# First layer's maximum pass of a two-layer attention kernel: one maximum over two banks in place of two over one

## The chip, the cores and the metric

One core of a Trainium2 chip runs the whole program. The time is device microseconds (us) of one execution. The figures of the kernel before are three plain runs and one profiled execution; its trace has 75059 instructions.

## What is computed

Eight images of 64 x 64 positions with 64 channels go through two attention layers. For each image, with n = 4096 positions:

```
xf = x.reshape(b, n, c)
f = xf @ wf + bf;  g = xf @ wg + bg;  hh = xf @ wh + bh      # layer 0, f and g have 8 channels
s = einsum('bnk,bmk->bnm', g, f)
x = gamma * softmax(s) @ hh + x
q, k, v = projections of x with 64 channels each             # layer 1
x = gamma1 * softmax(q @ k^T) @ v + x
```

The softmax of layer 0 needs the maximum of each row of s before its exponentials. This kernel finds it in a pass of its own, the maximum pass, with a cheaper product (72 contraction rows instead of 75), and that pass is what the change is about.

## The kernel before, in words

PSUM is held as two tensors of four banks, each 128 partitions by 512 f32: score_banks and sum_banks. The work of layer 0 on one image is cut into NCH = 4 chunks (q = 0 to 3) of 1024 query positions. chunk0 on PE (L435), ACT (L591) and DVE (L734) walks a chunk in T = 32 steps (i = 0 to 31), each over 128 key positions. The order of every engine's instructions is written out by hand, and semaphores couple the engines.

One step on PE is, in order:

- scores0 (L380): two matmuls of 512 columns (L383) into two banks of score_banks. ACT then takes the exponential of the 1024 columns in one instruction (L600) into one of eight slots of e_whole.
- max_pass_tiles (L361): two matmuls of 512 columns (L366), each into its own bank of sum_banks (banks 2 and 3), for a chunk that comes later. DVE takes the maximum of each bank with block_max (L724, instruction at L727).
- values0 (L394): f32 matmuls (L401, recorded as four per step) that add the weighted values of step i - 5 (LAG0 = 5) into bank 0. In one step of four the row sums of that slot go to PE too (sum_of, L414, matmuls at L417, into bank 1); in the other three POOL adds the slot to a running sum (L289, L292).

The maximum pass has 8 tiles of 512 keys per block of 128 queries (ATN = 8), 64 per chunk; a step of the loop does tiles 2(i mod 4) and 2(i mod 4) + 1 of one block. A tile's matmul waits on the semaphore a_used, which DVE raises by one per maximum; GpSimd gives FREE_A = 4 credits at the start. In the loop only banks 2 and 3 are used (banks=2), in the pass ahead of the first image (L506 to L508 on PE, L809 to L813 on DVE, 80 tiles) all four banks (banks=4). DVE waits on a_ready, one per matmul.

Some steps are different:

- q = 0, i = 0 to 4: no values0, since the lag of 5 isn't filled. These steps are scores and maximum tiles alone. The first values0 is in step i = 5.
- q > 0: steps 0 to 4 carry the last five values of the chunk before. Step 5 has no values0. Step 6 has turn0 (L421): PE transposes the sums that ACT (v_sb, L589) and DVE (d_sb, L732) have copied, and DVE turns them into the attention output with attention0 (L761: L767, L768, L769) once it has done the maxima of step 6. Steps 7 and 8 have two values0 each, and the first waits for L769 since it writes bank 0 again.
- i = 23: DVE writes the row maxima of the next chunk with split_max (L749, five small instructions), after its maxima.
- i = 26 (MROW_AT): after values0, max_rows (L369) waits for every maximum issued so far and for split_max, and writes banks 2 and 3 with eight small matmuls (L376); ACT copies them out (L584).
- i = 27: the maximum tiles come last in the step, behind values0 and a wait for that copy (L459 to L461), so that the tiles of step 27 and of step 28 have only the two score matmuls of step 28 between them.

Layer 1 (scores1 L463, values1 L473, steps1 L546/L654/L875) has a maximum of 1024 columns over two banks per step already, in one DVE instruction (L880). It isn't touched.

Of the kernel before, what the change touches and what calls it, by code (L numbers as in the profile page):

```python
# [21 lines left out]
AX_X = mybir.AxisListType.X  # L22
ds = bass.ds

P = 128
BANK = 512
# [4 lines left out]
def attention_pair_kernel(nc, x, wf, bf, wg, bg, wh, bh, gamma0, wq, bq, wk, bk, wv, bv, gamma1, out):  # L31
    B, H, W, C = x.shape
    N = H * W
# [4 lines left out]
    CH = 2 * BANK  # L38
# [9 lines left out]
    RT = T // BPC  # L48
    ATN = N // BANK
    ATS = T * ATN  # L50
    U0 = 8
# [4 lines left out]

    FREE_ST, FREE_A, FREE_E0, FREE_S1, FREE_E1 = 2, 4, U0, 2, U1
    FREE = 1
# [16 lines left out]
    with ExitStack() as ctx:  # L75
# [239 lines left out]
        def _(pe):  # L315
# [44 lines left out]

            def max_pass_tiles(ahead, blk, js, banks=2):  # L361

                image, par, q = ahead
                for j in js:
                    pe.wait_ge(a_used, image * ATS + q * TILES + blk * ATN + j + 1 + FREE_A - banks)
                    nc.tensor.matmul(sum_banks[:, (2 + j % banks) % 4, :], g_tr[0:KS, par, ds(q * CH + blk * P, P)],  # L366
                                     f_tr[0:KS, par, j * BANK:(j + 1) * BANK], start=True, stop=True).then_inc(a_ready, 1)

# [62 lines left out]
            def after(image, par, q):  # L431

                return (image, par, q) if q < NCH else (image + 1, 1 - par, q - NCH)

            def chunk0(image, par, q):  # L435
# [3 lines left out]
                for i in range(T):  # L439
                    scores0(image, par, q, i)  # L440
                    if q == 0 and i == 0:
                        pe.wait_ge(y_ready, image * NCH + FREE)
                    tiles = range(2 * (i % 4), 2 * (i % 4) + 2)
                    if i < LAST:
# [12 lines left out]
                    if i == MROW_AT:  # L457
                        max_rows(after(image, par, q + 1), 2 * (MROW_AT - LAST + 1))
                    elif i == MROW_AT + 1:  # L459
                        pe.wait_ge(mrow_sb, image * NCH + q + 2)  # L460
                        max_pass_tiles(after(image, par, q + 2), (i - LAST) // 4, tiles)  # L461
# [44 lines left out]
            for chunk, blocks in ((0, BPC), (1, EARLY)):  # L506
                with pe.Fori(0, blocks) as blk:
                    max_pass_tiles((0, 0, chunk), blk, range(ATN), 4)  # L508
            max_rows((0, 0, 0), EARLY * ATN)
# [174 lines left out]
        def _(dve):  # L684
# [38 lines left out]

            def block_max(chunk, blk, js, banks=2):  # L724
                for j in js:
                    dve.wait_ge(a_ready, chunk * TILES + blk * ATN + j + 1)
                    nc.vector.reduce_max(tile_max[:, blk, j:j + 1], sum_banks[:, (2 + j % banks) % 4, :], AX_X  # L727
                                         ).then_inc(a_used, 1)

# [4 lines left out]
            def chunk0(image, par, q):  # L734
                ahead = image * NCH + q + 1
                for i in range(T):
                    tiles = range(2 * (i % 4), 2 * (i % 4) + 2)
                    if i < LAST:
                        block_max(ahead, EARLY + i // 4, tiles)
                    else:  # L740
                        block_max(ahead + 1, (i - LAST) // 4, tiles)
                    if q > 0 and i == LAG0:
                        copy_sums0(image, q - 1)
                    if q > 0 and i == TURN_AT:
                        attention0(image, q - 1)
                    if i == LAST - 1:
                        split_max(ahead, (par * NCH + q + 1) % (2 * NCH))
# [61 lines left out]
            with dve.Fori(0, BPC) as blk:  # L809
                block_max(0, blk, range(ATN), 4)  # L810
            split_max(0, 0)
            with dve.Fori(0, EARLY) as blk:
                block_max(1, blk, range(ATN), 4)  # L813
            START += 2 * LINK_PIECES + LINK_MAX
# [134 lines left out]
```

## Time and profile before

| | us |
|---|---|
| plain runs, median of 3 | 5068.23 |
| plain runs, lowest and highest | 5059.25, 5069.01 |
| profiled execution, its own time | 5049.6 |
| its span, first to last instruction | 5047.8 |
| mean granted TensorE clock in it | 0.943 of full speed |

The page's first part gives the busy time of each engine and its share of the span. PE is the tensor engine's matmuls, PEld its weight loads, which run beside matmuls. A line of the costliest groups reads: source line, engine, operation, output<-input, shapes, count, then busy us and mean ns of one, then the idle time in front of them and who ended it. A line of the timeline reads: start us, length us, engine, source line, operation, tiles, count of merged instructions, and in brackets the idle time before it and what released it. Matmul ends are modelled, so the start of the next one tells more than the length of one. A line of the windows reads: stretch, its length, busy us (and count) of PE, PEld, DVE, ACT and POOL, then PEclk, the granted TensorE clock as a share of full speed (full speed is 2.4 GHz, 0.5 is 1.2 GHz), the DMA share and GB/s.

### The profile page before, as it was taken

Reading aid. Unit: us, or ns where it says so; the run is one execution under the profiler, and the core shown is the slowest. Engines: PE = TensorE matmul, PEld = TensorE weight load, DVE = VectorE, ACT = ScalarE, POOL = GpSimd, SP = SyncE. Lnnn points to the kernel's source line nnn. Section 1 sums busy time; section 2 is a strip of 40 time slices with the busy share of each in tenths; the row PEclk is TensorE's granted clock in tenths of the full one; section 3 lists DMA queues with packets and bytes.
Section 4 is the critical chain, followed back from the end, with each engine's and each line's share of the span. In section 5 each row is a group of like instructions: output and inputs, shape, how many; then the busy total and the mean of one; then the engine's idle time right before and its main releaser. Section 6 shows DMA issues by size and latency. Waiting matters only on the chain.

```text
span 5047.8 us, 75059 instructions
## 1 busy us (share of the span) xinstructions
PE 4836.0 (96%) x21608; PEld 1511.7 (30%) x21608; DVE 3533.9 (70%) x6722; ACT 2755.7 (55%) x3752; POOL 1831.4 (36%) x821
## 2 busy tenths in 40 slices
PE   7999999999999999999999999999999999999999
PEld 3224222242222422233222422224222242222422
DVE  6566876678765787558866588665885568866687
ACT  2555655556555565546655466554664546655465
POOL 2772017710177003760037600475005740067300
PEclk6998999989999899998989989998998989999899
DMA  0000000000000000000000000000000000000000
GB/s 26 1 9 17 0 8 1 9 17 0 9 1 9 17 0 9 1 9 17 0 10 1 18 9 0 9 1 24 2 0 10 1 26 0 0 9 3 24 0 8
DMA packets 13506, 40.03 MB, mean 8 GB/s; under 512 B 2620, under 2 KB 2620, under 8 KB 10812
## 3 DMA queue, kind: packets, MB, share of 16 engines
q1 hardware_dynamic: 13244, 36.78, 2.4%
q8 instruction: 135, 2.21, 0.2%
q14 instruction: 127, 1.04, 0.1%
HBM read 19.99 MB, written 8.39 MB: 6 GB/s over the span
## 4 chain that ended last, share of the span: by engine, by line
PE 61%; DVE 24%; issue 11%; ACT 2%; DVEq 1%; SPq 0%; ACTq 0%; DMA 0%
PE sum_banks L401 20%; DVE chunk_max L880 15%; PE score_banks L383 10%; PE sum_banks L366 9%; PE score_banks L468 5%; PE score_banks L469 4%; PE sum_banks L480 3%; PE sum_banks L417 3%; PE score_banks L541 2%; PE score_banks L340 2%; DVE tile_max L727 2%; DVE exp_bias L883 2%; ACT e_whole L659 1%; DVE inv_sum L862 1%; PE score_banks L325 1%
## 5 line engine op out<-in xcount | busy, mean ns | idle before, releaser
L727 DVE TENSOR_REDUCE tile_max<-sum_banks 128x1 f32<-128x512 f32 (+1 forms) x2128 | 1363.4, 686 | 914.3 <-PE sum_banks L366 914.1
L292 POOL TENSOR_TENSOR e_sum<-e_sum,e_whole 128x1024 f32<-128x1024 f32 x704 | 1655.4, 2351 | 429.7 <-ACT e_whole L600 409.2
L600 ACT ACTIVATE e_whole<-score_banks,no_bias 128x1024 f32<-128x1024 f32 x1024 | 1141.4, 1115 | 1105.2 <-PE score_banks L383 1103.1
L659 ACT ACTIVATE e_whole<-score_banks,exp_bias,down 128x1024 f32<-128x1024 f32 x1024 | 1233.3, 1204 | 764.7 <-DVE exp_bias L883 764.7
L880 DVE TENSOR_REDUCE chunk_max<-score_banks 128x1 f32<-128x1024 f32 x1024 | 1251.2, 1222 | 227.1 <-PE score_banks L469 212.9
L401 PE MATMUL sum_banks<-e_whole,proj 128*64 128x512 f32 x4096 | 1109.2, 627 | 27.0 <-DVE att L769 27.0
L480 PE MATMUL sum_banks<-e_whole,v_scaled 128*64 128x512 f32 x4096 | 1095.2, 617 | 6.6 <-DVE v_scaled L870 6.6
L289 POOL TENSOR_TENSOR e_sum<-e_whole 128x1024 f32<-128x1024 f32 x32 | 75.2, 2349 | 2231.3 <-ACT e_whole L600 2231.3
L468 PE MATMUL score_banks<-k_high,q_split 128*128 128x512 f16 x2048 | 800.4, 391 | 70.7 <-ACT e_whole L659 38.8
L469 PE MATMUL score_banks<-k_low,q_split 128*128 128x512 f16 x2048 | 790.3, 386 | 0.0
L366 PE MATMUL sum_banks<-f_tr,g_tr 72*128 72x512 bf16 x2128 | 693.2, 400 | 30.6 <-DVE tile_max L727 15.8
L383 PE MATMUL score_banks<-g_tr,f_tr 75*128 75x512 bf16 x2048 | 642.0, 396 | 12.1 <-issue 11.0
L468 PEld LDWEIGHTS score_banks<-k_high,q_split 128*128 (+1 forms) x2048 | 200.0, 98 | 1025.7 <-ACT e_whole L659 674.4
L401 PEld LDWEIGHTS sum_banks<-e_whole,proj 128*64 128x64 f32 x4096 | 214.3, 136 | 470.8 <-issue 437.3
L480 PEld LDWEIGHTS sum_banks<-e_whole,v_scaled 128*64 128x64 f32 x4096 | 207.5, 135 | 453.8 <-issue 453.8
L383 PEld LDWEIGHTS score_banks<-g_tr,f_tr 75*128 75x128 bf16 x2048 | 130.8, 99 | 659.0 <-ACT e_whole L600 464.9
L366 PEld LDWEIGHTS sum_banks<-f_tr,g_tr 72*128 72x128 bf16 (+1 forms) x2128 | 209.5, 100 | 396.1 <-DVE tile_max L727 140.8
L883 DVE TENSOR_SCALAR exp_bias<-chunk_max,neg_down 128x1 f32<-128x1 f32 x1024 | 219.2, 214 | 36.1
L469 PEld LDWEIGHTS score_banks<-k_low,q_split 128*128 (+1 forms) x2048 | 203.6, 99 | 126.9 <-issue 9.5
L659 ACT ACTIVATION_READ_ACCUMULATOR e_whole<-score_banks,exp_bias,down 128x1 f32 x1024 | 196.2, 192 | 0.0
L417 PE MATMUL sum_banks<-e_whole,ones_w 128*32 128x256 f32 x2048 | 164.6, 393 | 0.0
L541 PE MATMUL score_banks<-x_tr,w1s 65*128 65x512 f32 x128 | 111.9, 1069 | 12.3 <-DVE w1s L843 12.3
(100 smaller groups left out, 2074.3 us busy)
## 6 DMA issues: line engine op xcount, KB each, us to landing
x_in<-in_x_dram SPq DMA_DIRECT2D x19, 1024.0 KB, 4.9
out_dram<-x_mid SPq DMA_DIRECT2D x32, 256.0 KB, 2.2
k_high<-k_high SPq DMA_DIRECT2D x32, 128.0 KB, 2.2
k_low<-k_low SPq DMA_DIRECT2D x32, 128.0 KB, 2.2
gammas<-in_L_conv_gamma_dram SPq DMA_DIRECT2D x2, 0.5 KB
w<-in_L_conv_wg_dram SPq DMA_DIRECT2D x1, 2.0 KB
w<-in_L_conv_bg_dram SPq DMA_DIRECT2D x1, 0.0 KB
w<-in_L_conv_wf_dram SPq DMA_DIRECT2D x1, 2.0 KB
```

The costliest lines, as they stand in the source:

```text
L292: nc.gpsimd.tensor_tensor(acc, acc, e_whole[:, i % U0, :], ALU.add).then_inc(e_added, 1)
L366: nc.tensor.matmul(sum_banks[:, (2 + j % banks) % 4, :], g_tr[0:KS, par, ds(q * CH + blk * P, P)], f_tr[0:KS, par, j * BANK:(j + 1) * BANK ...
L383: mm = nc.tensor.matmul(score_banks[:, 2 * (i % 2) + h, :], f_tr[0:KM, par, i * P:(i + 1) * P], g_tr[0:KM, par, q * CH + h * BANK:q * CH + ...
L401: mm = nc.tensor.matmul(sum_banks[half * C:(half + 1) * C, 0, :], proj[:, par, i, GFW:PW], e_whole[:, i % U0, half * BANK:(half + 1) * BAN ...
L468: nc.tensor.matmul(bank, q_split[:, ds(i * P, P)], k_high[:, col:col + BANK], start=True, stop=False)
L469: mm = nc.tensor.matmul(bank, q_split[:, ds(i * P, P)], k_low[:, col:col + BANK], start=False, stop=True)
L480: mm = nc.tensor.matmul(sum_banks[half * C:(half + 1) * C, j, :].rearrange("c (k n) -> c k n", n=P), v_scaled[:, u // NCH, j, :], half_of_ ...
L600: nc.scalar.activation(e_whole[:, i % U0, :].rearrange("p (a n) -> p a n", a=2), score_banks[:, 2 * (i % 2):2 * (i % 2) + 2, :], ACT.Exp, ...
L659: nc.scalar.activation(e_whole[:, u, :].rearrange("p (a n) -> p a n", a=2), score_banks[:, 2 * (u % 2):2 * (u % 2) + 2, :], ACT.Exp, bias= ...
L727: nc.vector.reduce_max(tile_max[:, blk, j:j + 1], sum_banks[:, (2 + j % banks) % 4, :], AX_X).then_inc(a_used, 1)
L880: chain.link(nc.vector.reduce_max(chunk_max[:, odd, j:j + 1], score_banks[:, 2 * (u % 2):2 * (u % 2) + 2, :] .rearrange("p a n -> p (a n)" ...
L883: nc.vector.tensor_scalar(exp_bias[:, u:u + 1], chunk_max[:, odd, j:j + 1], neg_down[:, 0:1], None, ALU.mult).then_inc(bias_ready, 1)
```

## The change

The unit of the maximum pass becomes a pair of banks. PE writes two matmuls into a pair and raises a_ready once, after the second; both stand behind one wait on a_used. DVE takes one maximum over the 1024 columns of the pair and raises a_used once. ATN falls from 8 to 4 and FREE_A from 4 to 2. In the loop there is one pair (pairs=1, banks 2 and 3), so each pair of matmuls waits for the maximum of the step before; in the pass ahead of the first image there are two pairs (pairs=2, all four banks).

```diff
@@ -46,7 +46,7 @@
     TR = BANK // P
     RND = T // TR
     RT = T // BPC
-    ATN = N // BANK
+    ATN = N // CH
     ATS = T * ATN
     U0 = 8
     U1 = 2 * NCH
@@ -54,7 +54,7 @@
     LAG1 = 7
     STEPS0, STEPS1 = NCH * T, T * NCH
 
-    FREE_ST, FREE_A, FREE_E0, FREE_S1, FREE_E1 = 2, 4, U0, 2, U1
+    FREE_ST, FREE_A, FREE_E0, FREE_S1, FREE_E1 = 2, 2, U0, 2, U1
     FREE = 1
 
     EARLY = U0 // 4
@@ -358,13 +358,17 @@
                         mm.then_inc(ready, 1)
 
 
-            def max_pass_tiles(ahead, blk, js, banks=2):
+            def max_pass_tiles(ahead, blk, js, pairs=1):
 
                 image, par, q = ahead
                 for j in js:
-                    pe.wait_ge(a_used, image * ATS + q * TILES + blk * ATN + j + 1 + FREE_A - banks)
-                    nc.tensor.matmul(sum_banks[:, (2 + j % banks) % 4, :], g_tr[0:KS, par, ds(q * CH + blk * P, P)],
-                                     f_tr[0:KS, par, j * BANK:(j + 1) * BANK], start=True, stop=True).then_inc(a_ready, 1)
+                    pe.wait_ge(a_used, image * ATS + q * TILES + blk * ATN + j + 1 + FREE_A - pairs)
+                    pair = 1 - j % pairs
+                    for h in range(2):
+                        mm = nc.tensor.matmul(sum_banks[:, 2 * pair + h, :], g_tr[0:KS, par, ds(q * CH + blk * P, P)],
+                                              f_tr[0:KS, par, (2 * j + h) * BANK:(2 * j + h + 1) * BANK],
+                                              start=True, stop=True)
+                    mm.then_inc(a_ready, 1)
 
             def max_rows(ahead, tiles_ahead):
 
@@ -440,7 +444,7 @@
                     scores0(image, par, q, i)
                     if q == 0 and i == 0:
                         pe.wait_ge(y_ready, image * NCH + FREE)
-                    tiles = range(2 * (i % 4), 2 * (i % 4) + 2)
+                    tiles = [i % 4]
                     if i < LAST:
                         max_pass_tiles(after(image, par, q + 1), EARLY + i // 4, tiles)
                     elif i != MROW_AT + 1:
@@ -455,7 +459,7 @@
                     elif i >= LAG0 and (q == 0 or i > TURN_AT):
                         values0(image, par, q, i - LAG0)
                     if i == MROW_AT:
-                        max_rows(after(image, par, q + 1), 2 * (MROW_AT - LAST + 1))
+                        max_rows(after(image, par, q + 1), MROW_AT - LAST + 1)
                     elif i == MROW_AT + 1:
                         pe.wait_ge(mrow_sb, image * NCH + q + 2)
                         max_pass_tiles(after(image, par, q + 2), (i - LAST) // 4, tiles)
@@ -505,7 +509,7 @@
                 pe.wait_ge(gt_sb, (image + 1) * NCH)
             for chunk, blocks in ((0, BPC), (1, EARLY)):
                 with pe.Fori(0, blocks) as blk:
-                    max_pass_tiles((0, 0, chunk), blk, range(ATN), 4)
+                    max_pass_tiles((0, 0, chunk), blk, range(ATN), 2)
             max_rows((0, 0, 0), EARLY * ATN)
             def image_steps(image, par):
                 for q in range(NCH):
@@ -721,11 +725,12 @@
                     nc.vector.tensor_copy(half_of_blocks(r, 1), score_banks[C:P, r, :]
                                           .rearrange("c (k n) -> c k n", n=P)).then_inc(xt_dve[layer], 1)
 
-            def block_max(chunk, blk, js, banks=2):
+            def block_max(chunk, blk, js, pairs=1):
                 for j in js:
+                    pair = 1 - j % pairs
                     dve.wait_ge(a_ready, chunk * TILES + blk * ATN + j + 1)
-                    nc.vector.reduce_max(tile_max[:, blk, j:j + 1], sum_banks[:, (2 + j % banks) % 4, :], AX_X
-                                         ).then_inc(a_used, 1)
+                    nc.vector.reduce_max(tile_max[:, blk, j:j + 1], sum_banks[:, 2 * pair:2 * pair + 2, :]
+                                         .rearrange("p a n -> p (a n)"), AX_X).then_inc(a_used, 1)
 
             def copy_sums0(image, q):
                 dve.wait_ge(pv0_done, (image * NCH + q + 1) * T + FREE_E0)
@@ -734,7 +739,7 @@
             def chunk0(image, par, q):
                 ahead = image * NCH + q + 1
                 for i in range(T):
-                    tiles = range(2 * (i % 4), 2 * (i % 4) + 2)
+                    tiles = [i % 4]
                     if i < LAST:
                         block_max(ahead, EARLY + i // 4, tiles)
                     else:
@@ -807,10 +812,10 @@
                 assert chain.n == LINK_PIECES
             rebase(START + 2 * LINK_PIECES)
             with dve.Fori(0, BPC) as blk:
-                block_max(0, blk, range(ATN), 4)
+                block_max(0, blk, range(ATN), 2)
             split_max(0, 0)
             with dve.Fori(0, EARLY) as blk:
-                block_max(1, blk, range(ATN), 4)
+                block_max(1, blk, range(ATN), 2)
             START += 2 * LINK_PIECES + LINK_MAX
 
             def image_steps(image, par):
```

## Rows read from the trace of the kernel before

**Rows 1.** page, busy time of each engine

```profile
PE 4836.0 (96%) x21608; PEld 1511.7 (30%) x21608; DVE 3533.9 (70%) x6722; ACT 2755.7 (55%) x3752; POOL 1831.4 (36%) x821
```

**Rows 2.** page, costliest groups: the one-bank maximum and layer 1's two-bank maximum

```profile
L727 DVE TENSOR_REDUCE tile_max<-sum_banks 128x1 f32<-128x512 f32 (+1 forms) x2128 | 1363.4, 686 | 914.3 <-PE sum_banks L366 914.1
...
L880 DVE TENSOR_REDUCE chunk_max<-score_banks 128x1 f32<-128x1024 f32 x1024 | 1251.2, 1222 | 227.1 <-PE score_banks L469 212.9
```

**Rows 3.** timeline, an ordinary step of a chunk at full clock

```profile
755.74 0.60 PE L366 MATMUL sum_banks<-f_tr,g_tr 72*128 72x512 bf16 x2
...
756.16 1.29 DVE L727 TENSOR_REDUCE tile_max<-sum_banks 128x1 f32<-128x512 f32 x2 [0.69 <-PE sum_banks L366]
...
756.27 1.08 PE L401 MATMUL sum_banks<-e_whole,proj 128*64 128x512 f32 x4
...
757.51 0.32 PEld L366 LDWEIGHTS sum_banks<-f_tr,g_tr 72*128 72x128 bf16 x2
757.72 0.60 PE L366 MATMUL sum_banks<-f_tr,g_tr 72*128 72x512 bf16 x2
```

**Rows 4.** timeline, the pass ahead of the first image

```profile
62.00 4.28 DVE L727 TENSOR_REDUCE tile_max<-sum_banks 128x512 f32 x7 [1.00 <-PE sum_banks L366]
62.74 0.10 PEld L366 LDWEIGHTS sum_banks<-f_tr,g_tr 72*128 x1 [0.73 <-DVE tile_max L727]
62.75 0.39 PE L366 MATMUL sum_banks<-f_tr,g_tr 72*128 72x512 bf16 x1 [0.24 <-DVE tile_max L727]
```

**Rows 5.** timeline, steps without values, first image, low clock

```profile
114.36 1.06 PE L366 MATMUL sum_banks<-f_tr,g_tr 72*128 72x512 bf16 x2
...
115.03 1.29 DVE L727 TENSOR_REDUCE tile_max<-sum_banks 128x1 f32<-128x512 f32 x2 [3.79 <-PE sum_banks L366]
...
116.07 1.06 PE L366 MATMUL sum_banks<-f_tr,g_tr 72*128 72x512 bf16 x2
...
123.88 1.98 PE L401 MATMUL sum_banks<-e_whole,proj 128*64 128x512 f32 x4
```

**Rows 6.** timeline of PE, the same steps of the last image, full clock

```profile
4434.62 0.60 PE L366 MATMUL sum_banks<-f_tr,g_tr 72*128 72x512 bf16 x2 [1.15 <-DVE x_mid L917]
...
4441.56 0.65 PE L401 MATMUL sum_banks<-e_whole,proj 128*64 128x512 f32 x2
```

**Rows 7.** timeline, steps 5 to 7 of a chunk with q > 0

```profile
815.08 0.60 PE L366 MATMUL sum_banks<-f_tr,g_tr 72*128 72x512 bf16 x2
...
815.49 1.29 DVE L727 TENSOR_REDUCE tile_max<-sum_banks 128x1 f32<-128x512 f32 x2 [1.69 <-PE sum_banks L366]
...
816.70 0.41 DVE L732 COPY d_sb<-sum_banks 128x256 f32<-128x256 f32 x1
...
817.03 1.28 DVE L727 TENSOR_REDUCE tile_max<-sum_banks 128x1 f32<-128x512 f32 x2
```

**Rows 8.** timeline, the same place further on

```profile
819.88 3.62 PE L401 MATMUL sum_banks<-e_whole,proj 128*64 128x512 f32 x8 [1.12 <-DVE att L769]
...
824.40 1.94 PE L401 MATMUL sum_banks<-e_whole,proj 128*64 128x512 f32 x8
```

**Rows 9.** timeline, steps 26 to 28 of a chunk

```profile
790.12 1.29 DVE L727 TENSOR_REDUCE tile_max<-sum_banks 128x1 f32<-128x512 f32 x2 [0.69 <-PE sum_banks L366]
...
791.54 0.63 PE L376 MATMUL sum_banks<-ident_b,g_stack 128*75 128x128 bf16 x8 [0.23 <-DVE tile_max L727]
...
793.98 2.48 DVE L727 TENSOR_REDUCE tile_max<-sum_banks 128x1 f32<-128x512 f32 x4 [2.57 <-PE sum_banks L366]
...
795.64 1.08 PE L401 MATMUL sum_banks<-e_whole,proj 128*64 128x512 f32 x4
```

**Rows 10.** windows of 20 us from an image's first value matmul (images 0, 6, 7)

```profile
123.88:143.88 20.00, 20.00 (x63) 4.39 (x63) 8.71 (x14) 7.06 (x7) 12.45 (x6) 0.67 0.00 0
...
3824.67:3844.67 20.00, 20.00 (x51) 4.05 (x52) 6.79 (x12) 5.85 (x6) 10.54 (x5) 0.51 0.00 0
4441.56:4461.56 20.00, 20.00 (x94) 5.12 (x94) 12.28 (x20) 10.46 (x10) 18.37 (x9) 1.00 0.00 1
```

## The prediction

> **What bounds the kernel now.** I read the page's busy times first: PE is busy 96% of the span and DVE 70% [rows 1]. So the change, which takes work off DVE and none off PE, has nothing to win where PE never waits. The costliest groups give the two prices of a maximum: 686 ns for 512 columns, and in layer 1, which has the new shape already, 1222 ns for 1024 [rows 2]. The timeline of an ordinary step shows what matters most. PE starts the two tile matmuls at 755.74 and again at 757.72, a step of 1.98 us with PE issuing all the way, and DVE starts the first maximum 0.42 us after the first matmul, ends the pair 1.29 us later and then sits idle 0.69 us for PE [rows 3]. In layer 0 PE sets the time and DVE follows. A lighter DVE is worth nothing there; a PE made to wait costs all of the wait.
>
> **What the change does to the coupling.** Two things. The maximum starts after the second matmul, one issue spacing later (0.22 us at full clock, 0.43 us at half). And the loop keeps one pair of banks, so both matmuls of a step wait for the whole maximum of the step before, where the first one waited only for the first half. Pair against pair, start to end, DVE goes from 1.29 to 1.22 us, and since it starts 0.22 us later its pair ends 0.15 us later than now.
>
> The way round is then: first matmul, 0.22 to the second, 0.42 to the start of the maximum, 1.22 for it, then the release. In the pass ahead of the first image a maximum begins at 62.00 and lasts 0.68 us, and the weight load that waited for it starts at 62.74, its matmul at 62.75 [rows 4]: 0.06 for the release, 0.01 to the matmul. Sum 1.93 us at full clock. At half clock the first matmul of a pair to the first maximum is 0.67 us [rows 5], so the way round is 0.43 + 0.67 + 1.22 + 0.07 = 2.39 us. Wherever two tile pairs follow each other on PE in less than that, PE now stands still for the difference.
>
> **Ordinary steps: nothing, by 0.05 us.** They are 1.98 us apart, the way round is 1.93. The cover is the value matmuls between (1.0 us). Steps with row sums, and all steps with values at half clock, are longer still. Some 18 of 32 steps in each of the 32 chunks stand on this margin, nearly 600; if the way round were 0.05 us over the step, it would cost 30 us. I take nothing and keep 30 for the range. At i = 23 DVE's five small instructions follow the maximum; step 24 carries row sums, which cover them.
>
> **Steps 0 to 5 of q = 0 (eight times).** No values lie between the pairs of steps 0 to 5, five gaps. At half clock the pairs start 1.71 us apart, and 9.52 us pass from the first pair to the first value matmul [rows 5]. Now each gap is 2.39: 5 x 0.68 = +3.4 us. Seven of the eight images fall to half clock in or before these steps; I price them all so: 23.8 us. The last image stayed at full clock and took 6.94 us [rows 6]. With pairs 1.93 us apart PE would stand still for more than half of each gap, where it now stands still for a third of 1.2 us, and I expect the clock to fall as in the others: two gaps at 1.93, three at 2.39, 1.0 to the values, about 12.0 in all, +5.0 us. Below: if the clock held, 5 x (1.93 - 1.2) = +3.6.
>
> What follows in that image goes slow too. In the 20 us behind the first value matmul the clock averages 0.67 in the first image, 0.51 in the seventh and 1.00 in the last [rows 10]; the mean of all eight such windows is 0.80, so they hold 82 us at half clock, 11.7 for each of the seven that fell. Eight value matmuls take 3.62 us slow and 1.94 fast [rows 8], so a slow us wastes 0.46: +5.4 us for the last image. For the others no net change, though each image draws its length anew (2 to 20 us).
>
> **Steps 5 to 7 of q > 0 (24 times).** Step 5 has no values. The second maximum of step 5 ends at 816.78, DVE's copy of the sums and the two maxima of step 6 follow, the latter from 817.03 to 818.31 [rows 7], then L767 to L769, and the value matmuls at 819.88, after 1.12 us of idle PE that L769 ends [rows 8]. Now: the maximum of step 5 from 815.49 + 0.22 = 815.71 to 816.93; tiles of step 6 at 817.00 and 817.22; maximum 817.64 to 818.86. That is 0.55 us later on the chain that PE already waits for: 24 x 0.55 = +13.2 us. Queued behind the waiting tiles are the turn's transposes, whose inputs are ready by then, and the scores of step 7; ACT has room.
>
> **Step 26 (32 times).** max_rows waits for all maxima: they end at 791.41, L376 starts at 791.54 [rows 9]. All maxima now end 0.15 later: +4.8 us. **Steps 27 and 28 (32 times).** Only two score matmuls lie between their tiles. Already now both tiles of step 28 wait, and the value matmuls start at 795.64. Now: maximum from 793.98 + 0.22 = 794.20 to 795.42, tiles 795.49 and 795.71, and the values 0.31 later, as in an ordinary step [rows 3], at 796.02 against 795.64 [rows 9]: 32 x 0.38 = +12.2 us.
>
> **Pass ahead of the first image.** DVE is the bound: seven maxima take 4.28 us, a spacing of 0.60 [rows 4]. Two pairs of banks remain, so work overlaps. A 1024 maximum would be spaced by 1.22 less the overlap of 0.08, 1.14; by the way round at half clock, a pair for each of two, 2.39 / 2 = 1.19. Against 1.20 to 1.21: between -2.5 and 0 for 40 pairs. I take -1.0, since most of the stretch is at half clock. The Trainium skill, Perfetto Trace Analysis, section Optimizing Scalar/DVE Operations, gives about 125 ns of DVE time per PSUM instruction; by it 40 fewer instructions would give 5 us and the sum would be 4 lower. The rows say 0.06 us, since two maxima overlap by more than that.
>
> **Clock falls inside chunks.** At one of the 24 places above (the one of rows 8) the clock was at half for the first eight value matmuls, 1.68 us lost. PE now waits longer there; from one in 24 I go to three, +3.4, and hold 0 and 24 x 1.68 = 40 as the ends.
>
> **Sum.** 23.8 + 5.0 + 5.4 + 13.2 + 4.8 + 12.2 - 1.0 + 3.4 = +66.8 us, against the profiled execution's own 5049.6: 5116.4. The median of plain runs is 18.6 above that execution. I read part of that as the last image's luck, so the 5.4 and the 1.6 by which it costs more than the others don't come on top of the median: 5068.2 + 59.8 = **5128.0 us**, 1.2% slower.
>
> **Rivals.**
>
> 1. *The margin in ordinary steps is not there* (a longer maximum in layer 0, a later release). For: 0.05 us is two or three digits of the trace's last place, and 600 steps hang on it. Against: layer 1's duration has little spread and the restart of a waiting matmul costs 0.01. Price 30 us: 5158. In the same direction speaks the Trainium skill, Perfetto Trace Analysis, section Matmuls: independent groups should rotate through banks so that the evacuation overlaps the next matmuls, which the loop no longer does. Chance 0.14.
>
> 2. *The clock falls at most places with q > 0.* Price 40 - 3.4: 5165. For: one fell already. Against: 23 didn't, with 1.12 us of idle each. Chance 0.08.
>
> 3. *Stalls within slow stretches are half paid for*: the clock comes back at its own time whatever PE has done, so the 3.4 us per image replace slow work. Price: 27 x 0.46 = 12 less, 5116. Chance 0.15.
>
> 4. *Not slower.* One mechanism: slow clock. The profiled run averages 0.943, about 575 us at half clock. PE's longer waits shift when it rises; the gain is 0.46 us for each slow us saved, so from 130 us saved on it cancels the 60: 5068 or less. The stretches behind the images' starts hold only 82 us, worth 38, so these alone don't reach it; it would need the stretches between the layers too. Chance 0.05.
>
> That the code would not do what it says I exclude: with pairs=1 the pair is always banks 2 and 3, and the credits (2, and one pair held back) admit one maximum at a time.
>
> **How the numbers follow.** The forecast has 0.58, rival 3 0.15, rivals 1 and 2 0.22 together, rival 4 0.05. The range from 5096 (rival 3, no clock falls, luck of 15 us with the lengths) to 5165 (rival 1 or 2 alone) leaves out rival 4 and the sum of 1 and 2. A measurement of this kernel tells about 0.2%, 10 us, from no change. Rival 4 splits into faster by more, 0.03, and within, 0.02, to which the low tail of the forecast adds 0.01; slower by more has the rest, 0.94.
>
> **What would show it.** One L727 per step of about 1.22 us, 1064 in all. In ordinary steps L366 still 1.98 apart, with the weight load starting 0.05 or less ahead of its matmul instead of 0.21. Gaps of 2.4 us between pairs at the start of every image, the last too. From the tiles of step 5 to the first values of step 7, 5.35 us for 4.80 [rows 7, 8]. From the start of the first maximum of step 27 to the values of step 28, 1.82 us for 1.66, and 0.15 more ahead of L376. Wrong if steps of 2.0 us and more appear (rival 1), or if the mean clock rises.

## The result and the profile after

The changed kernel takes **5183.56 us** (median of 4 runs, 5159.24 to 5195.01) where the kernel before took 5063.74 in the same session: a ratio of **1.0235**, 95% interval 1.0207 to 1.0263. The forecast was 5128.0 in a range of 5096 to 5165. The sign was right; the loss is twice the forecast's (119.8 us for 59.8), and the time lies outside the range.

The profiled execution of the changed kernel took 5174.86 us, its span is 5172.9 (5047.8 before) and the mean granted clock 0.932 (0.943). Its page, busy time of each engine and three of the costliest groups (columns: busy us, mean ns of one, idle before them and what ended it):

```profile
PE 4888.8 (95%) x21608; PEld 1508.9 (29%) x21608; DVE 3488.7 (67%) x5658; ACT 2753.4 (53%) x3752; POOL 1830.4 (35%) x821
...
L732 DVE TENSOR_REDUCE tile_max<-sum_banks 128x1 f32<-128x1024 f32 (+1 forms) x1064 | 1300.8, 1224 | 1078.9 <-PE sum_banks L368 1078.0
...
L405 PE MATMUL sum_banks<-e_whole,proj 128*64 128x512 f32 x4096 | 1137.5, 642 | 42.5 <-DVE att L774 42.5
...
L368 PE MATMUL sum_banks<-f_tr,g_tr 72*128 72x512 bf16 x2128 | 683.3, 404 | 94.5 <-DVE tile_max L732 87.7
```

DVE has 1064 maxima of 1.22 us in place of 2128 [rows 1, 2], as forecast. They are busy 63 us less (1300.8 for 1363.4), but DVE as a whole only 45 us less: some of the saving went into another instruction, shown below. PE's waits went up. Its busy time went up by 53 us with the same 21608 matmuls, which is slow clock (700 us of the span at half clock instead of 579, by the clock records).

**An ordinary step** (timeline, after; start, us, engine, line). It answers to [rows 3].

```profile
775.62 0.60 PE L368 MATMUL sum_banks<-f_tr,g_tr 72*128 72x512 bf16 x2
776.26 1.23 DVE L732 TENSOR_REDUCE tile_max<-sum_banks 128x1 f32<-128x1024 f32 x1 [0.76 <-PE sum_banks L368]
...
777.54 0.17 PEld L368 LDWEIGHTS sum_banks<-f_tr,g_tr 72*128 72x128 bf16 x2 [0.27 <-DVE tile_max L732]
777.61 0.60 PE L368 MATMUL sum_banks<-f_tr,g_tr 72*128 72x512 bf16 x2
```

The tiles are 1.99 and 1.98 us apart as before, and the weight load now starts 0.07 ahead of its matmul instead of 0.21 (0.05 or less was forecast). The margin held.

**The start of an image** (timeline of PE, after, second image). It answers to [rows 5, 6].

```profile
746.77 0.60 PE L368 MATMUL sum_banks<-f_tr,g_tr 72*128 72x512 bf16 x2 [1.15 <-DVE x_mid L922]
...
748.69 0.61 PE L368 MATMUL sum_banks<-f_tr,g_tr 72*128 72x512 bf16 x2 [0.89 <-DVE tile_max L732]
...
750.62 1.04 PE L368 MATMUL sum_banks<-f_tr,g_tr 72*128 72x512 bf16 x2 [0.89 <-DVE tile_max L732]
...
752.97 1.03 PE L368 MATMUL sum_banks<-f_tr,g_tr 72*128 72x512 bf16 x2 [0.47 <-DVE tile_max L732]
755.33 1.03 PE L368 MATMUL sum_banks<-f_tr,g_tr 72*128 72x512 bf16 x2 [0.47 <-DVE tile_max L732]
757.68 1.03 PE L368 MATMUL sum_banks<-f_tr,g_tr 72*128 72x512 bf16 x2 [0.47 <-DVE tile_max L732]
```

The gaps are 1.92 and 1.93 at full clock and 2.35 at half, as worked out (1.93 and 2.39).

**Where the 125.1 us of span went.** I took the length of every one of the 1024 steps in both traces (from a step's scores to the next step's) and subtracted.

| place | forecast | measured |
|---|---|---|
| ordinary steps | 0 | 0.0 |
| the five gaps at the start of q = 0 (steps 1 to 5 by this count) | 28.8 | 28.5 |
| step 0 (-2.0) and steps 6 to 12 (+15.3) of q = 0, more half clock | 5.4 | 13.4 |
| steps 5 to 8 of q > 0, clock falls included | 16.6 | **60.5** |
| step 26 | 4.8 | 4.9 |
| steps 27 and 28 | 12.2 | 11.8 |
| pass ahead of the first image | -1.0 | +1.9 |
| start of the kernel up to that pass | 0 | +5.6 |
| everything else | 0 | -1.5 |
| sum | 66.8 | 125.1 |

One row is far off: steps 5 to 8 of q > 0, where the values wait for a chain of small instructions on DVE (the reciprocal L772, the multiply L773 and the attention output L774). The 24 places are of two kinds. Timeline of the changed kernel, first a chunk of the bad kind (POOL's two additions are rows of POOL's own timeline):

```profile
837.03 2.35 POOL L292 TENSOR_TENSOR e_sum<-e_sum,e_whole 128x1024 f32<-128x1024 f32 x1 [0.62 <-ACT e_whole L604]
...
839.18 0.20 DVE L772 RECIPROCAL inv_sum<-sum_banks 128x8 f32<-128x8 f32 x1
839.42 2.41 DVE L773 TENSOR_SCALAR inv_gam<-inv_sum,gammas 128x8 f32<-128x8 f32 x1
839.46 2.34 POOL L292 TENSOR_TENSOR e_sum<-e_sum,e_whole 128x1024 f32<-128x1024 f32 x1
841.86 0.69 DVE L774 TENSOR_TENSOR att<-sum_banks,inv_gam 128x512 f32<-128x512 f32 x1
...
842.70 3.25 PE L405 MATMUL sum_banks<-e_whole,proj 128*64 128x512 f32 x8 [2.77 <-DVE att L774]
```

and the next chunk, of the good kind:

```profile
913.12 2.35 POOL L292 TENSOR_TENSOR e_sum<-e_sum,e_whole 128x1024 f32<-128x1024 f32 x1 [0.62 <-ACT e_whole L604]
...
915.27 0.20 DVE L772 RECIPROCAL inv_sum<-sum_banks 128x8 f32<-128x8 f32 x1
915.51 0.23 DVE L773 TENSOR_SCALAR inv_gam<-inv_sum,gammas 128x8 f32<-128x8 f32 x1
915.56 2.39 POOL L292 TENSOR_TENSOR e_sum<-e_sum,e_whole 128x1024 f32<-128x1024 f32 x1
915.77 0.69 DVE L774 TENSOR_TENSOR att<-sum_banks,inv_gam 128x512 f32<-128x512 f32 x1
...
916.61 1.94 PE L405 MATMUL sum_banks<-e_whole,proj 128*64 128x512 f32 x8 [0.59 <-DVE att L774]
```

The same instruction, a multiply of 8 values in each of 128 partitions by a scale, takes 0.23 us or 2.41. When it takes 2.41 it ends 0.03 after the end of POOL's addition, which started 0.04 behind it. PE waits 2.77 us instead of 0.59 for the values, and the values then run slow (3.25 for 1.94). The windows of 8 us around the two places (PE, PEld, DVE, ACT, POOL busy with counts, then the granted clock):

```profile
837.00:845.00 8.00, 4.60 (x18) 1.96 (x20) 6.25 (x7) 2.48 (x3) 4.69 (x2) 0.81 0.00 1
911.00:919.00 8.00, 6.29 (x33) 2.48 (x30) 4.95 (x7) 3.72 (x4) 6.25 (x3) 1.00 0.01 2
```

The clock is at full (2.4 GHz) throughout the good one and at half (1.2) in part of the bad one. Over the chunks with q > 0, half clock rose from 3.4 us to 68.3, and all of it lies behind 12 of the 13 long multiplies. At the 13th the multiply takes 2.41 us and PE waits 2.77 as well, and the clock stays at full (two lines of the timeline, then the window of 8 us around them):

```profile
4147.93 2.41 DVE L773 TENSOR_SCALAR inv_gam<-inv_sum,gammas 128x8 f32<-128x8 f32 x1
...
4151.22 1.51 PE L405 MATMUL sum_banks<-e_whole,proj 128*64 128x512 f32 x6 [2.77 <-DVE att L774]
```

```profile
4145.50:4153.50 8.00, 4.59 (x22) 1.90 (x23) 6.26 (x7) 2.50 (x3) 4.68 (x2) 1.00 0.01 2
```

At the other 12 the clock falls 1.7 to 3.8 us after the multiply has begun, never before it.

The multiply was too long in the kernel before, too. Kernel before, the same chain as timeline (it lies between [rows 7] and [rows 8]), and then the row of the multiply's line over the whole run (ns, min/median/max):

```profile
816.63 2.35 POOL L292 TENSOR_TENSOR e_sum<-e_sum,e_whole 128x1024 f32<-128x1024 f32 x1 [0.62 <-ACT e_whole L600]
818.23 0.20 DVE L767 RECIPROCAL inv_sum<-sum_banks 128x8 f32<-128x8 f32 x1
818.46 0.55 DVE L768 TENSOR_SCALAR inv_gam<-inv_sum,gammas 128x8 f32<-128x8 f32 x1
...
819.04 0.69 DVE L769 TENSOR_TENSOR att<-sum_banks,inv_gam 128x512 f32<-128x512 f32 x1
819.06 2.35 POOL L292 TENSOR_TENSOR e_sum<-e_sum,e_whole 128x1024 f32<-128x1024 f32 x1
```

```profile
L768 DVE TENSOR_SCALAR inv_gam<-inv_sum,gammas x32: 230/549/554, 202.8 to 4722.3; 128x8 f32<-128x8 f32 x32
```

It starts 1.83 us into POOL's addition and ends 0.03 behind it (816.63 + 2.35 = 818.98, 818.46 + 0.55 = 819.01). The next addition starts 0.60 after the multiply did, so there was a hole of 0.05 us (819.01 to 819.06) that it always went through. It took 0.55 at all 24 places with q > 0 and 0.23 at the 8 places behind an image's last chunk, where POOL adds nothing (its last addition had ended 7 us earlier). In the changed kernel it arrives 0.03 behind the end of one addition and 0.05 ahead of the next, and it was held at 13 of the 24 places.

### The profile page after: what moved, and what is told of

The parts are those of the page before. It is cut to its first block, busy times and chain, and to the rows that moved or that the text cites. A ratio compares the mean times of both kernels' runs of the same rounds, so it can differ in the third digit from the quotient of the medians.

```text
span 5172.9 us, 71767 instructions
## 1 busy us (share of the span) xinstructions
PE 4888.8 (95%) x21608; PEld 1508.9 (29%) x21608; DVE 3488.7 (67%) x5658; ACT 2753.4 (53%) x3752; POOL 1830.4 (35%) x821
## 4 chain that ended last, share of the span: by engine, by line
PE 61%; DVE 25%; issue 10%; ACT 2%; DVEq 1%; SPq 0%; ACTq 0%; DMA 0%
PE sum_banks L405 20%; DVE chunk_max L885 15%; PE sum_banks L368 10%; PE score_banks L387 10%; PE score_banks L472 5%; DVE tile_max L732 4%; PE score_banks L473 3%; PE sum_banks L421 3%; PE sum_banks L484 3%; PE score_banks L545 2%; PE score_banks L340 2%; DVE exp_bias L888 2%; PE score_banks L528 1%; ACT e_whole L663 1%; DVE inv_sum L867 1%
## 5 line engine op out<-in xcount | busy, mean ns | idle before, releaser
L732 DVE TENSOR_REDUCE tile_max<-sum_banks 128x1 f32<-128x1024 f32 (+1 forms) x1064 | 1300.8, 1224 | 1078.9 <-PE sum_banks L368 1078.0
L405 PE MATMUL sum_banks<-e_whole,proj 128*64 128x512 f32 x4096 | 1137.5, 642 | 42.5 <-DVE att L774 42.5
L368 PEld LDWEIGHTS sum_banks<-f_tr,g_tr 72*128 72x128 bf16 (+1 forms) x2128 | 181.9, 100 | 461.3 <-DVE tile_max L732 334.5
L279 POOL TENSOR_TENSOR g_stack<-piece,ones_b 128x768 bf16<-128x768 bf16 x30 | 54.0, 1800 | 200.4 <-DVE piece L795 200.4
```

The source lines that it names most:

```text
L368: mm = nc.tensor.matmul(sum_banks[:, 2 * pair + h, :], g_tr[0:KS, par, ds(q * CH + blk * P, P)], f_tr[0:KS, par, (2 * j + h) * BANK:(2 * j ...
L405: mm = nc.tensor.matmul(sum_banks[half * C:(half + 1) * C, 0, :], proj[:, par, i, GFW:PW], e_whole[:, i % U0, half * BANK:(half + 1) * BAN ...
```

## The experiments

The theory to be tested is that this hold makes the excess. Its rivals: the chain is simply later and every 0.1 us of it is paid; or the slow clock comes first and the long steps from it.

**First group: take the multiply out of either kernel, and delay it in the kernel before.** `pair_fused` is the changed kernel with gamma folded into the ones that PE multiplies for the row sums (so gamma must not be 0), `single_fused` the same edit on the kernel before:

```diff
+            chain.link(nc.vector.reciprocal(inv_gamma0[:, :], gammas[:, 0:1]))
+            nc.vector.tensor_scalar(ones_w[:, :], ones_w[:, :], inv_gamma0[:, 0:1], None, ALU.mult).then_inc(w_ready, 1)
...
-                chain.link(nc.vector.tensor_scalar(inv_gam0[:, :], inv_sum0[:, :], gammas[:, 0:1], None, ALU.mult))
...
-                                        inv_gam0[:, :].rearrange("p (a k) -> p a k", a=2).unsqueeze(3)
+                                        inv_sum0[:, :].rearrange("p (a k) -> p a k", a=2).unsqueeze(3)
```

> The pair kernel, with gamma folded into the ones of the row sums, so that DVE's small multiply between the reciprocal and the attention output is gone. In the trace of the pair kernel this multiply took 2.41 us at 13 of the 24 places with q > 0 and 0.23 at the others, and it began within 0.05 us of the border between two GpSimd additions. Theory A (the multiply needs something that GpSimd's addition holds, and loses that race half of the time; the wait of PE of 2.8 us then brings the clock down): step 7 takes 3.64 us at all 24 places, clock falls inside chunks with q > 0 go from 68 us to under 10, and the kernel is 55 to 62 us faster than the pair kernel, near +1.2% over the kernel before. Theory B (the clock falls come from the pair's longer waits by themselves): the falls stay, only 24 x 0.25 = 6 us are won, +2.2% over before.

> The kernel before with the same fold. There the multiply took 0.55 us at all 24 places and ended with GpSimd's addition. Theory A: the chain behind step 6 is 0.55 us shorter at each, 24 x 0.55 = 13 us faster, 0.3%. Theory B: 24 x 0.23 = 6 us, within 0.2% of before.

Measured: pair_fused 5102.87, ratio to before 1.0089 (1.0059 to 1.0118). The ratio falls from 1.0235 to 1.0089, some 74 us (55 to 62 had been expected), with one instruction of 8 elements a partition gone. In the traces 63.1 us of it lie in steps 6 to 8 of q > 0; most of the rest lies where neither edit reaches, at the start of the kernel and in layer 1. Step 7 takes 3.62 us at all 24 places and no chunk with q > 0 has any half clock. single_fused: 5042.15, 0.9974 (0.9957 to 0.9992); step 7 is 0.59 us shorter at 23 places and 2.27 at the one where the clock had fallen. PE's wait for `att` (columns: total us, times, longest), first in the changed kernel:

```profile
PE sum_banks L405 <- DVE att L774: 42.5, 24, 2.8
```

and in single_fused:

```profile
PE sum_banks L401 <- DVE att L772: 12.9, 24, 0.5
```

The two fused kernels differ by 60.7 us, and that is the price of the change with the multiply out of the way. In steps 6 to 8 of q > 0 their difference is 13.2 us (pair_fused 2.6 below before, single_fused 15.8 below), which is 24 x 0.55, the term of the forecast.

`single_delay_a` and `single_delay_b` are the kernel before with its single maxima; only copies out of a PSUM bank, whose result nobody reads, stand ahead of the multiply: 128 columns in a, 512 and 256 in b. The edit of b:

```diff
+                nc.vector.tensor_copy(scr[:, 0, 0:512], sum_banks[:, 0, 0:512])
+                nc.vector.tensor_copy(scr[:, 1, 0:256], sum_banks[:, 0, 0:256])
                 chain.link(nc.vector.tensor_scalar(inv_gam0[:, :], inv_sum0[:, :], gammas[:, 0:1], None, ALU.mult))
```

> The kernel before with one more DVE copy out of PSUM of 128 columns (about 0.2 us) ahead of the multiply. Theory A: the multiply starts later and still ends with GpSimd's addition, so its length falls from 0.55 to about 0.35 and the time does not change. Theory B, or any plain chain: +0.2 x 24 = 5 us, and the multiply keeps its 0.55.

> The kernel before with two more DVE copies out of PSUM, of 512 and 256 columns (about 0.9 us), ahead of the multiply, so that it starts behind the border of GpSimd's additions, which lies 0.52 to 0.60 us after its present start. The kernel keeps its single maxima. Theory A: the multiply takes 2.0 to 2.4 us at all 24 places, PE waits over 3 us at each, the clock falls at most of them, and the kernel is 24 x (2.4 + 1.7) = some 100 us slower, 2.0%. Theory B: 24 x 0.9 = 22 us slower, 0.4%, few falls.

Measured: a 5059.36, ratio 1.0006 (0.999 to 1.0022); b 5189.51, 1.0255 (1.0216 to 1.0294). The row of the multiply's line in each (ns, min/median/max), a first:

```profile
L770 DVE TENSOR_SCALAR inv_gam<-inv_sum,gammas x32: 220/342/347, 198.6 to 4721.9; 128x8 f32<-128x8 f32 x32
```

```profile
L771 DVE TENSOR_SCALAR inv_gam<-inv_sum,gammas x32: 218/2028/2035, 203.8 to 4866.0; 128x8 f32<-128x8 f32 x32
```

In a the multiply starts 0.20 later, lasts 0.21 less, and costs nothing: it ends with POOL's addition as before, and the rival by which every delay is paid falls. In b it starts 0.34 behind the start of POOL's next addition and is held at all 24 places:

```profile
837.58 0.69 DVE L769 COPY scr<-sum_banks 128x512 f32<-128x512 f32 x1
838.19 0.41 DVE L770 COPY scr<-sum_banks 128x256 f32<-128x256 f32 x1
838.19 2.34 POOL L293 TENSOR_TENSOR e_sum<-e_sum,e_whole 128x1024 f32<-128x1024 f32 x1
838.52 2.03 DVE L771 TENSOR_SCALAR inv_gam<-inv_sum,gammas 128x8 f32<-128x8 f32 x1
840.58 0.69 DVE L772 TENSOR_TENSOR att<-sum_banks,inv_gam 128x512 f32<-128x512 f32 x1
...
841.42 3.68 PE L402 MATMUL sum_banks<-e_whole,proj 128*64 128x512 f32 x8 [3.54 <-DVE att L772]
```

Without one pair of maxima, a multiply that starts 0.94 us later (838.52 less 837.58) costs as much as the whole change. Its steps 7 and 8 hold 139 us more than before (some 100 had been expected), its chunks with q > 0 195 us of half clock (3.4 before). All other steps of those chunks are as long as before to within 0.1 us in their sum. The clock came second: the steps ahead of the held multiply are as long as before, the clock falls 0.6 to 3.6 us after its start at all 24 places, and the changed kernel has places where the multiply is held and the clock stays up (1 of 13, and 3 of 16 in the repeat below).

No run moves POOL's additions. That it is they which hold the multiply is read from its end, which lies 0.03 us behind the end of an addition at each of the 24 places of before, a, b and m_turn below and at each held place of the changed kernel, wherever it starts; and from the places without an addition, where it takes 0.23.

**Second group: one part of the change at a time.** Four kernels have the paired maximum in some steps only. PE waits once for both tiles of the step before, DVE takes one maximum over both banks; the handshake keeps a count per tile and costs 0.07 us more per pair than the changed kernel's.

```diff
+                if pair:
+                    dve.wait_ge(a_ready, chunk * TILES + blk * ATN + js[1] + 1)
+                    nc.vector.reduce_max(tile_max[:, blk, js[0]:js[1] + 1], sum_banks[:, 2:4, :], AX_X
+                                         ).then_inc(a_used, 2)
+                    return
```

The condition for `pair`: m_start `q == 0 and i <= 5`, m_turn `q > 0 and i in (5, 6, 7)`, m_tail `i in (26, 27, 28)`, m_ord every step that none of these names (steps 5 to 7 of q > 0 excluded too).

> The kernel before with pairs (both matmuls behind one wait for both maxima of the step before, one DVE instruction over the two banks) only in ordinary steps: single maxima in steps 0 to 5 of q = 0, steps 5 to 7 of q > 0, steps 26 to 28 and in the pass ahead of the first image. Theory: the way round of 1.93 us fits the step of 1.98, so no change, -5 to +5 us. Rival (every step pays a little): +20 to +40 us.

> Pairs only in steps 0 to 5 of q = 0. Theory: the gaps between the pairs grow to 2.39 us at half clock, +28 us in eight images, and the half clock lasts longer into the steps with values (it does in seven of eight images of the pair kernel), +15: 43 us slower, 0.85%. Rival (the longer half clock of the pair kernel was chance): +28 us, 0.55%.

> Pairs only in steps 5 to 7 of q > 0. Theory A (DVE's multiply meets the border of two GpSimd additions and loses at about half of the places): 40 to 60 us slower, about 1.0%, with multiplies of 2.4 us and clock falls in the trace. Theory B (the coupling alone): 24 x 0.41 = 10 us slower, 0.2%.

> Pairs only in steps 26 to 28 of every chunk. Both theories: 32 x (0.15 + 0.37) = 17 us slower, 0.33%, with no clock fall. With more than 25 us something in these steps is not understood.

| | us | ratio (interval) | in the trace |
|---|---|---|---|
| m_ord | 5070.29 | 1.0014 (0.9997 to 1.0032) | step 1.99 for 1.98 |
| m_start | 5108.29 | 1.0087 (1.0065 to 1.011) | gaps +31.8, steps 6 to 11 +29 |
| m_turn | 5197.54 | 1.0277 (1.0252 to 1.0302) | steps 6 to 8 +138, 24 of 24 held |
| m_tail | 5081.3 | 1.0026 (1.0005 to 1.0046) | steps 26 and 28 +21.1 |

m_ord fits the margin: 0.07 us more in the handshake against a cover of 0.05 leaves 0.02, and the step grew by 0.01. m_tail fits the forecast with the longer handshake: +0.22 and +0.44 a step for 0.15 and 0.37. (Its trace also has 26 us more in steps 6 to 12 of q = 0, which it doesn't touch; the medians are 12.2 apart.) m_turn is the expensive one, and I had expected 40 to 60 us for it. Timeline of m_turn at the chain, and the row of its multiply:

```profile
846.53 0.20 DVE L781 RECIPROCAL inv_sum<-sum_banks 128x8 f32<-128x8 f32 x1
...
846.67 2.34 POOL L295 TENSOR_TENSOR e_sum<-e_sum,e_whole 128x1024 f32<-128x1024 f32 x1
...
846.76 2.27 DVE L782 TENSOR_SCALAR inv_gam<-inv_sum,gammas 128x8 f32<-128x8 f32 x1
849.07 0.69 DVE L783 TENSOR_TENSOR att<-sum_banks,inv_gam 128x512 f32<-128x512 f32 x1
```

```profile
L782 DVE TENSOR_SCALAR inv_gam<-inv_sum,gammas x32: 230/2274/2282, 209.4 to 4867.2; 128x8 f32<-128x8 f32 x32
```

The longer handshake puts the multiply 0.09 behind the start of the addition instead of 0.04 or 0.05 ahead of it, and it lost every time. So the parts don't add up to the change (138 against 60 for this one), and the reason is again the place of one start.

**Third group: the two halves of the coupling, and the change once more.** Both halves stand on single_fused, so that the multiply can't disturb them. `wait_whole` lets both tile matmuls wait for the whole step before and leaves DVE its two maxima; `start_late` lets DVE start when both tiles are there and leaves PE's waits.

```diff
+                    last = js[-1] if banks == 2 else j
+                    if banks == 4 or j == js[0]:
+                        pe.wait_ge(a_used, image * ATS + q * TILES + blk * ATN + last + 1 + FREE_A - banks)
```

```diff
-                    dve.wait_ge(a_ready, chunk * TILES + blk * ATN + j + 1)
+                    dve.wait_ge(a_ready, chunk * TILES + blk * ATN + (js[-1] if banks == 2 else j) + 1)
```

> The kernel before with gamma folded away (so that the race with GpSimd plays no part) and one half of the pair's coupling: in the loop both tile matmuls stand behind one wait for both maxima of the step before; the maxima stay two, each started by its own matmul. The way round is 0.42 + 1.29 + 0.07 = 1.78 us at full clock. Against the folded kernel without it: ordinary steps 0; step 6 of q > 0 and step 28 +0.22 each, 24 x 0.22 + 32 x 0.22 = 12 us; at the starts of the images, half clock, 2.03 for 1.71 us, 5 x 0.32 x 8 = 13 us: 25 us in all. If the loss of the pair comes from the merged instruction itself, 0.

> The folded kernel with the other half of the coupling: the maxima stay two and PE waits for each bank on its own, but DVE begins the first only when both matmuls are through, 0.22 us later at full clock and 0.43 at half. Against the folded kernel: step 26 +0.22 and step 28 +0.22, 32 x 0.44 = 14 us; step 6 of q > 0 +0.22, 5 us; starts of the images at half clock 5 x 0.3 x 8 = 13 us: 32 us in all. Together with the other half this should make up what the folded pair kernel lost against the folded single one, 60 us.

> The changed kernel once more, beside the others on one chip. Theory A: the multiply of DVE takes either 0.23 or 2.4 us, near half of 24 each, and not the same places as in the first trace; +2.0 to +2.6% over before. If the same places lose again, the border is not a matter of chance but of the phase in which each chunk stands.

> The folded single kernel again with more rounds. Theory A: faster than before by 13 to 16 us (the trace showed 0.59 us at each of 24 places), 0.25 to 0.3%. Rival (the first result was chance): within 0.1%.

Measured: wait_whole 5069.88 (1.0023, 1.0006 to 1.0039), start_late 5084.98 (1.0043, 1.0027 to 1.006), single_fused_again 5042.72 (0.9967, 0.9951 to 0.9983). So the longer wait costs 27.2 us and the later start 42.3; together 69.5, where both in one (pair_fused less single_fused, another session) cost 60.7. Neither half alone is the change. In the traces, steps 6 to 12 of q = 0 left out, the halves cost 28.0 and 38.0 us and the pair 55.9. The 10.1 between are, by an estimate, what the one maximum gives back: 1.22 us for 1.29 at 40 gaps, 48 steps 6 and 7 and 64 steps 26 and 28, 10.6 us. In start_late step 7 grew by 0.25 us, which I had not foreseen: the later start counts once in step 5 and again in step 6, so the first maximum of step 6 begins 0.45 us later than in single_fused.

pair_again is the changed kernel unaltered: 5178.15, 1.0229 (1.0197 to 1.0261). The row of its multiply, with that of the first trace of the changed kernel behind it:

```profile
L773 DVE TENSOR_SCALAR inv_gam<-inv_sum,gammas x32: 230/1319/2417, 215.3 to 4848.8; 128x8 f32<-128x8 f32 x32
```

```profile
L773 DVE TENSOR_SCALAR inv_gam<-inv_sum,gammas x32: 230/231/2416, 213.6 to 4849.5; 128x8 f32<-128x8 f32 x32
```

It was held at 16 of the 24 places, and not at the same ones as the 13. The program is the same, and in both traces the multiply starts 0.04 or 0.05 us ahead of POOL's addition: which of the two engines gets through is open each time, and it hangs on nanoseconds. The two traces together, by recorded starts: 41 to 45 ns ahead, held at 20 of 20 places; 46 to 48 ns, at 9 of 25; 49 and 50 ns, at 0 of 3. The median flips from 231 to 1319 ns for no other reason than that half of 32 has been reached.

## Why the prediction was wrong in one step and right in the others

**The view of what bounds the kernel** was right. Less work on DVE won nothing anywhere; each added wait of PE was paid.

**Way round and margin** (1.93, 2.39, cover 0.05): measured 1.93, 2.35, and ordinary steps cost 0.0. Rival 1 did not happen. **Steps 0 to 5 of q = 0**: 28.5 for 28.8; the second image shows 11.87 us from the first pair to the first values (746.77 to 758.64), where 12.0 had been worked out for the last. **Step 26, steps 27 and 28**: 0.15 and 0.37 us each for 0.15 and 0.38.

**The pass ahead of the first image** took 1.9 more instead of 1.0 less; its maxima start 1.14 us apart and 1.31 to 1.39 in turn, 1.24 in the mean, where I had taken 1.14 to 1.19. The 5.6 at the start of the kernel is slow clock in the first projection, whose 64 matmuls take 13.78 us instead of 10.67 the first time and 10.71 instead of 8.55 the second. It came in pair_again and in m_turn too (which has no pair there), and not in pair_fused, so it is not put down to the change.

**Steps 5 to 7 of q > 0: the step that failed.** The sum had 13.2 + 3.4 us here; measured were 60.5. The prediction carried the chain over as a block, "then L767 to L769", 0.55 us later and with every duration as it was. The shift was right: the fused kernels show 24 x 0.55. The durations were not. L768's 0.55 us was 0.23 of its own and 0.32 of waiting for POOL, and that wait changes when the chain moves against POOL's additions:

- where the multiply gets through it is shorter by 0.32, so the chain is late by 0.55 - 0.32 = 0.23. Measured from the tiles of step 5 to the values of step 7: 911.57 to 916.61, 5.04 us, 0.24 above the 4.80 of before, where the forecast had 5.35;
- where it is held it takes 2.18 more than where it gets through, and the slow clock that follows costs about as much again: 4.35 us for each of the 13 in the mean, 56.6 us in all. (24 x 0.23 + 56.6, less the 1.7 of the one clock fall that the kernel before had, is the table's 60.5 but for rounding.)

Without these 56.6 the span would have grown by 68.5, against a sum of 66.8. That they agree so well is luck: this place would then have cost 3.8 instead of 16.6, and slow clock elsewhere, at the start of the kernel and in q = 0, came out 13.6 above the forecast. With all 24 places held the growth would be, by the same 4.35 each, 173. The trace that was open before the prediction had the clue: 8 values took 0.55 us at 24 places and 0.23 at 8.

The Trainium skill, SBUF — State Buffer, section SBUF: two separate sides, says that of the engines only VectorE and GpSimd share a pair of SBUF ports, and that it is a lock: an instruction of GpSimd, or one of VectorE in a mode with two ports or with two inputs in SBUF, holds the pair until it ends, the one that starts first gets it, and the other waits for all of it. The trace agrees with the hold, until 0.03 us behind the end of POOL's addition at every held place. It doesn't agree on who gets the pair: by the recorded starts, the held multiplies of the changed kernel began 0.04 to 0.05 us before the addition. That L768 runs in a mode with two ports, and that ports are what the two share, no run here shows. By that rule the rival "the multiply arrives a moment behind POOL's next addition" could have been written down with its price, 24 x 2.2 us and the clock.

**Clock falls inside chunks** were forecast as three of 24 (3.4 us), for waits of PE made 0.55 longer. Such waits did not come up in any run, so this step of the working stays untested: PE stands idle for 1.47 us in steps 6 to 8 in the kernel before, for 1.70 where the multiply gets through (no fall at 11 and 8 places), for 1.44 in pair_fused (no fall at 24). At the held places it is 3.88, 2.77 of it in one wait. Rival 2 had a loss of that order (40 us) in the right place, but by a cause that is not the right one: its falls were to follow from the ordinary wait.

**What follows in q = 0**, steps 6 to 12, was 15.3 in the changed kernel, 8.5 in pair_again and 13.4 in pair_fused, for 5.4 forecast. Kernels whose first steps of q = 0 are unchanged scatter by -2.5 to +26 us in the same steps, so how much of this belongs to the change stays open. m_start's trace has +30 there, but its median is 39.2 above before's, only 7.4 more than its gaps. The working behind the 5.4 also has a wrong mean: the eight windows of 20 us average 0.745, not 0.80. The 82 us at half clock that it goes on with fit 0.745. **Rival 3** (stalls in slow stretches are half paid) is not borne out: the gaps cost 28.5 in full and nothing came back later. **Rival 4** would have needed less slow clock; there were 700 us of it instead of 579.

## What to carry to other kernels

When an instruction takes longer than its size explains, find out what holds it before you move it: its duration in the trace contains the wait, and it doesn't move along. Here DVE's 8 values took 0.23 us alone, 0.55 with the tail of a POOL addition and 2.41 with a whole one, and a shift of the chain by 0.55 us, which with the multiply at 0.23 would have cost 0.23 us a place, put it on the border of the next.

Take small operations off a chain that runs beside another engine's long ones: folding gamma into the ones of the row sums makes the kernel before 0.3% faster (5042.15 and 5042.72, ratios 0.9974 and 0.9967) and is the only version here that beats both kernels.

One maximum for two banks won nothing here: ordinary steps stayed as long as they were, since DVE waits for PE there, and the pass with two pairs took 1.9 us more. With a single pair, compare the way round (0.22 + 0.42 + 1.22 + 0.07) with the distance of the tile pairs at every place of the loop, and count those where it is longer.

## What the runs showed of the hardware that was not expected

- A small DVE operation from SBUF to SBUF can wait for a POOL addition whose recorded start is later: with DVE's start 0.04 to 0.05 us ahead of POOL's it went either way (13 and 16 of 24 held in the two traces of the changed kernel), with 0.09 behind (m_turn) and 0.34 behind (single_delay_b) it was held 24 times of 24. When DVE got through, POOL's addition took 2.39 instead of 2.35.
- The profile shows no idle time for it. The wait is inside the duration: 8 values at 0.23, 0.34, 0.55, 2.03, 2.27 and 2.41 us in these runs.
- PE waits of 2.77 us were followed by half clock at 12 of 13 and 13 of 16 places, waits of 3.54 us (single_delay_b) at 24 of 24.
- It is not only this line. Other one-source operations of DVE from SBUF have two durations as well, in the kernel before (ns, min/median/max):

```profile
L754 DVE TENSOR_SCALAR g_stack<-row_max x33: 184/418/425, 100.6 to 4696.5; 128x8 bf16<-128x8 f32 x33
```

```profile
L790 DVE CAST piece<-proj x30: 426/1572/1575, 25.2 to 4746.8; 128x512 bf16<-128x512 f32 x30
```

20 of the 30 casts of L790 take 1.57 us, each beside a POOL operation (L279), and the other 10, with none beside them, take 0.43. L754 takes 0.42 at 32 of 33 places, beside an addition of POOL, and 0.18 at the one without. The reciprocal ahead of the multiply, which reads PSUM, took 0.20 beside the same additions. Whether the casts are worth separating was not tried.
